# The decays of a state-space layer made in steps, its half-unit on TensorE with all projections in one run, and the next weights' copy moved to the front of ScalarE's half-unit

## The reference, cut to what matters

```python
xn = layernorm(x)
x = x + attention(xn) * silu(moe_ffn(xn))          # 16 heads of 128, linear attention; 8 experts and a shared one
xn = layernorm(x)
x = x + ssm(xn) * silu(quantised_ffn(xn))          # the second layer: the part that the change touches
```

```python
x_t, z_t, b_t, c_t, a_log = split(xn @ W_in.T)     # four projections of 2048 columns and one of 32
decay = exp(-exp(a_log))
def step(states, inp):
    states = states * decay + x_t outer b_t
    y_t = states . c_t + x_t * D
y = layernorm(y * silu(z_t)) * gamma + beta
return y @ W_out.T
```

## Time and profile before

| what | value |
|---|---|
| median of 3 runs | 1784.79 us |
| the profiled execution: its time, and its span from the first to the last instruction | 1785.17 us, 1783.4 us |
| TensorE busy | 1646.7 us (92%) |
| VectorE busy | 1159.3 us (65%) |
| ScalarE busy | 760.0 us (43%) |
| GpSimd busy | 665.3 us (37%) |
| mean granted clock of TensorE | 0.974 |
| batch 0: FFN1 from about 433, the SSM stage from about 496 to about 833 | us from the span's start |
| batch 1: FFN1 from about 1320, the SSM stage from about 1383 to about 1720 | us from the span's start |

### The profile page before, as it was taken

The page is one execution under the profiler, slowest core; times in us unless marked ns, Lnnn a source line. Parts: engine busy times, 40 slices in busy tenths (PEclk is TensorE's granted clock), DMA queues, the critical chain, the costliest instruction groups (busy, mean ns, idle before and its releaser), DMA issues.

```text
span 1783.4 us, 29629 instructions
## 1 busy us (share of the span) xinstructions
PE 1646.7 (92%) x11068; PEld 1364.0 (76%) x11068; DVE 1159.3 (65%) x2041; ACT 760.0 (43%) x1393; POOL 665.3 (37%) x500
## 2 busy tenths in 40 slices
PE   5997899898899999999969978998989999999988
PEld 3886677787788888787938866776868788888878
DVE  4333788663667788886743347886536677777767
ACT  4343445433344444444633434554334344444445
POOL 1453444200225544444515534441012244444535
PEclk9998999999999999999979989999999999999999
DMA  2333000000244434441023320100002443443400
GB/s 77 96 112 118 18 36 1 1 1 10 71 138 143 122 119 129 135 128 49 13 71 104 112 110 19 36 1 1 1 10 71 160 125 119 137 136 120 138 29 25
DMA packets 60062, 135.68 MB, mean 76 GB/s; under 512 B 8129, under 2 KB 12737, under 8 KB 59409
## 3 DMA queue, kind: packets, MB, share of 16 engines
q1 hardware_dynamic: 59920, 133.79, 23.8%
HBM read 130.81 MB, written 2.95 MB: 75 GB/s over the span
## 4 chain that ended last, share of the span: by engine, by line
PE 67%; DVE 12%; POOL 7%; issue 6%; ACT 5%; DMA 2%; SPq 1%; POOLq 0%; DVEq 0%; ACTq 0%
PE ps L549 31%; PE ps L606 6%; PE ps L868 4%; PE ps L645 4%; PE ps L892 4%; PE ps L830 3%; POOL silu_g L449 3%; PE ps L904 3%; PE ps L585 3%; POOL rb L467 2%; POOL fw_lo L434 2%; PE ps L879 2%; PE ps L747 2%; PE ps L748 2%; DVE hid L1343 2%
## 5 line engine op out<-in xcount | busy, mean ns | idle before, releaser
L549 PE MATMUL ps<-xnT_hi,w_in_hi 128*128 128x512 f32 x512 | 222.6, 435 | 0.2 <-issue 0.2
L549 PE MATMUL ps<-xnT_lo,w_in_hi 128*128 128x512 f32 x512 | 203.7, 398 | 0.0
L549 PE MATMUL ps<-xnT_hi,w_in_lo 128*128 128x512 f32 x512 | 202.8, 396 | 0.0
L467 POOL TENSOR_TENSOR rb<-ra,rb 128x512 f32<-128x512 f32 x80 | 117.5, 1469 | 205.1 <-DVE rb L1533 205.1
L425 POOL TENSOR_TENSOR w_in_lo<-w_raw,w_in_hi 128x1024 fp32r<-128x1024 f32 x32 | 83.8, 2620 | 274.5 <-ACT w_in_hi L950 274.5
L1343 DVE TENSOR_TENSOR hid<-ps,silu_g 128x512 f32<-128x512 f32 (+1 forms) x80 | 55.1, 689 | 170.2 <-POOL silu_g L449 106.0
L1654 DVE TENSOR_TENSOR_SCAN lmat<-dec,ident 128x512 f32<-128x512 f32 x128 | 161.3, 1300 | 0.0
L549 PE MATMUL ps<-xnT_hi,fw_hi 128*128 128x512 f32 x312 | 127.8, 410 | 17.3 <-DVE fw_lo L1361 9.8
L512 POOL TENSOR_TENSOR yt<-yg,sz 128x512 f32<-128x512 f32 x64 | 83.5, 1304 | 154.4 <-ACT sz L1261 143.9
L434 POOL TENSOR_TENSOR fw_lo<-fw_raw,fw_hi 128x512 fp32r<-128x512 f32 (+1 forms) x56 | 62.5, 1117 | 186.1 <-ACT fw_hi L980 135.5
L549 PE MATMUL ps<-xnT_hi,fw_lo 128*128 128x512 f32 x312 | 125.1, 401 | 0.0
(11 more groups left out here) (194 smaller groups left out, 4394.6 us busy)
## 6 DMA issues: line engine op xcount, KB each, us to landing
dec<-dec_dram SPq DMA_DIRECT2D x64, 512.0 KB, 4.0
w_raw<-in_w_in SPq DMA_DIRECT2D x32, 512.0 KB, 4.9
wdec<-dec_dram SPq DMA_DIRECT2D x128, 128.0 KB, 4.0
pdec<-dec_dram SPq DMA_DIRECT2D x128, 128.0 KB, 3.8
fw_raw<-in_fw SPq DMA_DIRECT2D x40, 384.0 KB, 3.2
w_raw<-in_w_qkv SPq DMA_DIRECT2D x8, 768.0 KB, 4.2
comb<-comb_dram SPq DMA_DIRECT2D x8, 512.0 KB, 3.8
w_out<-in_w_o SPq DMA_DIRECT2D x2, 2048.0 KB, 10.7
```

Of the source, the lines that this page charges most:

```text
L467: nc.gpsimd.tensor_tensor(rb[:, k], ra[:, k], rb[:, k], ALU.add).then_inc(a_rot.sem, 1)
L549: mm = nc.tensor.matmul(out, left(l, k), right(r, k), start=(j == 0), stop=(j == len(steps) - 1))
```

## The change

It has four parts. On SyncE the first pair's weights are sent ahead of the decays' tables. On GpSimd `decay_suffix` waits for `f_hid` ahead of each step, one step to a half-unit of FFN1; on VectorE `decay_prefix` is split, its small operations after half-unit 3 and its scans after half-units 4 and 5. On TensorE all four projections stand in one run, ahead of the transposes and all the fp32 matmuls. On ScalarE `ssm_prep` moves to the front of the even half-units of pairs 1 to 14, for pair 0 behind the copy of the transposed b; c's copy and the silu of z move ahead of the transposed x.

```diff
--- before.py
+++ after.py
@@ -382,6 +382,7 @@
                 for k in range(2, NF1):
                     ffn_weights(b, NF0 + k, a["fw1"][k].bitcast(F32))
 
+                weights(split_ssm(b, 0), a["w_in"][0], KT * XZBC)
                 sp.wait_ge(s_prep, 5 * (b + 1))
                 sp.dma_start(dec_dram[0], dec_t[:]).then_inc(dec_out, 16)
                 sp.dma_start(dec_dram[1], dec_p[:]).then_inc(dec_out, 16)
@@ -390,7 +391,8 @@
                 sp.wait_ge(dec_out, 48 * (b + 1))
                 for h in range(HP):
                     n = b * HP + h
-                    weights(split_ssm(b, h), a["w_in"][h], KT * XZBC)
+                    if h > 0:
+                        weights(split_ssm(b, h), a["w_in"][h], KT * XZBC)
                     if h == 2:
                         sp.wait_ge(o_mm.sem, o_mm.done(b * NC + NC - 1))
                         sp.dma_start(w_out[:], a["w_out"]).then_inc(w_out_in, 16)
@@ -493,10 +495,12 @@
 
                     w = dec_w[:].rearrange("p (c t) -> p c t", t=P)
                     pool.wait_ge(s_dec.sem, s_dec.done(b))
+                    pool.wait_ge(f_hid.sem, f_hid.done(2 * (b * NF + NF0)))
                     nc.gpsimd.memset(w[:, :, P - 1:P], 1.0)
                     nc.gpsimd.tensor_copy(w[:, :, 0:P - 1], dec_t[:].rearrange("p (c t) -> p c t", t=P)[:, :, 1:P]).then_inc(suffix_step, 1)
                     for k in range(SUFFIX - 1):
                         reach = 1 << k
+                        pool.wait_ge(f_hid.sem, f_hid.done(2 * (b * NF + NF0) + 1 + k))
                         pool.wait_ge(suffix_step, SUFFIX * b + k + 1)
                         nc.gpsimd.tensor_tensor(w[:, :, 0:P - reach], w[:, :, 0:P - reach], w[:, :, reach:P], ALU.mult).then_inc(suffix_step, 1)
                 decay_suffix()
@@ -911,18 +915,17 @@
                     if ahead:
                         project_x(u + 1)
                         project_b(u + 1)
+                        project_c(u + 1)
+                    project_z(u)
+                    if ahead:
                         x_turn(u + 1)
                     unit_intra(u)
-                    if not ahead:
-                        project_z(u)
-                        unit_from_states(u)
-                        return
-                    project_c(u + 1)
-                    b_turn(u + 1)
+                    if ahead:
+                        b_turn(u + 1)
                     unit_from_states(u)
-                    project_z(u)
-                    unit_scores(u + 1)
-                    unit_updates(u + 1)
+                    if ahead:
+                        unit_scores(u + 1)
+                        unit_updates(u + 1)
 
                 u = 2 * b * HP
                 for hf in range(2):
@@ -1269,6 +1272,9 @@
                 def ssm_unit(u):
                     h, hf = u // 2 - b * HP, u % 2
                     ahead = u < 2 * HP * (b + 1) - 1
+                    early = hf == 0 and 1 <= h and h + 1 < HP
+                    if early:
+                        ssm_prep(h + 1, (h + 1) % 2)
                     if ahead:
                         x_copy(u + 1)
                     if u > 2 * b * HP:
@@ -1276,12 +1282,12 @@
                     if not ahead:
                         return
                     b_copy(u + 1)
+                    c_copy(u + 1)
+                    z_silu(u)
                     xtok_copy(u + 1)
-                    if hf == 0 and h + 1 < HP:
-                        ssm_prep(h + 1, (h + 1) % 2)
-                    c_copy(u + 1)
                     btok_copy(u + 1)
-                    z_silu(u)
+                    if h == 0 and hf == 0:
+                        ssm_prep(1, 1)
                     if u < 2 * b * HP + NC:
                         c = u - 2 * b * HP
                         if c == 0:
@@ -1632,20 +1638,21 @@
                     hidden(b, NF0 + k, hf, f_silu, 2 * (b * NF + NF0 + k) + hf, together=last)
                     hidden_lo(b, NF0 + k, hf, s_gu[0:rows, k, 1:2], rows)
 
-                def decay_prefix():
+                def prefix_starts():
 
                     starts = dec_t[:].rearrange("p (c t) -> p c t", t=P)[:, :, 0:1]
                     dve.wait_ge(s_dec.sem, s_dec.done(b))
+                    nc.vector.memset(dec_s[:], 0.0).then_inc(s_prep, 1)
                     dve.wait_ge(suffix_step, SUFFIX * b + 1)
-                    nc.vector.memset(dec_s[:], 0.0).then_inc(s_prep, 1)
                     dve.wait_ge(s_prep, 5 * b + 1)
                     nc.vector.tensor_copy(dec_s[:].rearrange("p (c t) -> p c t", t=P)[:, :, 0:1], starts).then_inc(s_prep, 1)
                     dve.wait_ge(s_prep, 5 * b + 2)
                     nc.vector.memset(starts, 0.0).then_inc(s_prep, 1)
+
+                def prefix_scan(hf):
+                    toks = slice(hf * HALF, (hf + 1) * HALF)
                     dve.wait_ge(s_prep, 5 * b + 3)
-                    for hf in range(2):
-                        toks = slice(hf * HALF, (hf + 1) * HALF)
-                        nc.vector.tensor_tensor_scan(dec_p[:, toks], dec_t[:, toks], dec_s[:, toks], 0.0, ALU.mult, ALU.add).then_inc(s_prep, 1)
+                    nc.vector.tensor_tensor_scan(dec_p[:, toks], dec_t[:, toks], dec_s[:, toks], 0.0, ALU.mult, ALU.add).then_inc(s_prep, 1)
 
                 def decay_scan(u, h):
                     if h == 0:
@@ -1731,8 +1738,10 @@
                     ffn1_unit(u)
                     if u // 2 + 1 < NF1:
                         weights_lo1(b, u // 2 + 1, u % 2)
-                    if u == 1:
-                        decay_prefix()
+                    if u == 3:
+                        prefix_starts()
+                    if u in (4, 5):
+                        prefix_scan(u - 4)
                     if u >= 2 * NF1 - 2:
                         decay_scan(u0, u - (2 * NF1 - 2))
                 for hf in range(2):
```

## The result

The changed kernel took 1840.46 us (median of 6 runs, 1833.31 to 1853.59), the kernel before 1783.47 beside it (6 runs, 1782.47 to 1785.3): a ratio of 1.0332 (95% interval 1.0307 to 1.0356). It is slower by 57 us. Forecast were 1827.0 us in a range of 1798 to 1856: the sign, the mechanism and the range held, and the sum was 13.5 us too low.

What follows compares the result with a forecast made beforehand. The tensor engine, never kept waiting in the SSM stage, was taken to bound the kernel; the change puts a longer loop there. 1785.2 + 49.4 - 2.4 + 3.8 - 9.0 = 1827.0 us, range 1798 to 1856.

Steps and rivals of the forecast that it cites:

- The loop (part 2): SSM stage: early weights' copy waits for its transfer, closing a scans-to-scans loop of 22.54 us; 26 x 1.90 = +49.4.
- dec and wdec sent and landed, up to bTw: First loop step, after the even half-unit's scans: SyncE issues both, wdec lands in 4.0; 5.00 us.
- GpSimd's turn: Even half-unit's scans: GpSimd's y_sum takes its turn between the two scans; 1.2 us, bounds 0 and 1.28.
- Part 1: Tensor engine's order, SSM stage: one projection run instead of three saves 0.40 us per head; six unlooped heads give -2.4.
- my lower bound: Tensor engine's order: a saving of 0 if each new seam among 4-byte matmuls costs what an old one did.
- Part 3: First head of each batch: later weights' copy delays the next projections; +1.9 us per batch, +3.8, bounds 0 and 2.5.
- Part 4: FFN1: GpSimd's decays in steps save a net 4.5 us per batch, -9.0; bounds 2 and 7 per batch.
- The waits for xT: Expected sign: tensor engine waits at the x transposes of even half-units, 2.2 us, 26 times.
- That the copy costs nothing: Rival: SSM transfer early enough that the tensor engine sets the pace; 1767 us, chance 0.08.
- The light loop: Rival: SSM loop binds lightly, GpSimd's turn beside the scans; about 1791 or 1808 us, part below 1805 has chance 0.10.
- The longer loop: Rival: wdec and weights land later in the SSM loop, 23.3 us; about 1853 us, above 1848 has chance 0.08.
- The clock: Rival: granted clock falls in the new SSM waits; +2 to +4 us per head, 1880 to 1930, chance 0.04.

Runs made afterwards that it cites:

- e7: The changed kernel with the 16 affine sums of batch 0 standing two by two in the odd half-units only; 1837.60 us.
- e1: The changed kernel with SyncE sending the next head's weights a half-unit earlier, between the head's two half-units; 1781.56 us.
- e5: The kernel before with only the new half-unit order, ScalarE's weights' copy behind the c copy in all heads, decays in one block; 1774.89 us.
- e6: The changed kernel with the weights sent a half-unit earlier and ScalarE's weights' copy behind the c copy in every head; 1773.16 us.
- e3: The kernel before with only the decays in steps, one GpSimd product per FFN1 half-unit, prefix starts and scans later; 1776.61 us.
- e10: The changed kernel with mt's products ahead of the x transposes and run twice in even half-units of heads 1 to 14; 1843.26 us.
- e4: The kernel before with only ScalarE's copy of the next weights put first in the even half-unit, heads 2 to 15; 1908.55 us.

## Why the prediction was right, and where 13 us are missing

**The loop (part 2) held, member by member.** The means over the 24 heads of the changed kernel in which both ends of the loop are in the trace, beside the forecast's steps, in us:

| step | forecast | measured |
|---|---|---|
| dec and wdec sent and landed, up to bTw | 5.00 | 5.36 |
| bTw and scans, odd half-unit | 2.94 | 2.94 |
| SyncE's queue ahead of the weights | 2.88 | 2.99 |
| landing, to the copy's start | 4.90 | 4.94 |
| copy, x, y square, b | 2.65 | 2.55 |
| gap, bTw and scans, even half-unit | 2.99 | 3.04 |
| GpSimd's turn beside these scans | 1.20 | 1.18 |
| sum | 22.56 (in the text 22.54) | 23.00 |

In batch 1, heads 2 to 14 took 22.55 us each (two half-units, mean); the forecast was 22.54. That it meets to 0.01 is luck: measured from scans to scans, single heads of that batch took 21.7 to 24.4, and the forecast's steps sum to 22.56. That the steps meet one by one is not. GpSimd's turn, an estimate between 0 and 1.28, shows in the rows: the two scans took 3.47 instead of 2.33, and GpSimd's y_sum beside them 2.19 instead of 1.28. The Trainium skill, GPSIMD Engine Reference, section Specifications, has GpSimd share its path to SBUF with vector instructions that read two SBUF inputs. The scans read dec and the constant, both in SBUF, and these rows agree; bTw, which reads PSUM and one SBUF input, took 0.69 with GpSimd at work and without. The same skill's fit for a transfer (DMA: Bandwidth & Descriptors, section Anatomy of one DMA), from which the forecast worked out an estimate of 3.2 us, is one for GpSimd's queue. It doesn't carry over to this transfer on SyncE's queue, which took 4.8.

**The step that failed is the first one of the loop, in batch 0.** There heads 2 to 14 took 23.33 us, 0.8 more than in batch 1. In eight of them the scans' end was followed by bTw after 6.08 us, because what the vector engine does in between (cTp, yg, mt, two affine sums, state updates) takes longer than wdec's landing; the rows 723.37 to 729.45 above show it without a gap. My step took wdec's landing as what ends last and looked at no half-unit of the vector engine with an affine sum in it. Less the 5.00 of the other sixteen, eight times 1.09 make 8.7 us, of which e7 showed 7.5 in the step and 3 in the time (about 6 against its own batch 1). Three more times in batch 0 SyncE sent the weights 0.4 to 1.4 us late (2.7 in sum). Its rows show there that sending itself took longer: 2.53 and 1.99 us for the two pieces of wdec instead of 1.12, and 1.68 for those of pdec instead of 1.23. Why is open.

**Part 1 was a quarter of its size.** The term of 0.20 per half-unit measured 0.05 (half-units of e1 and e5, from 10.15 + 10.49 to 10.10 + 10.44 us). Two beginnings of runs went, as said, but my lower bound, that new seams cost what old ones did, was nearer than the value I took. In the 26 heads that the loop sets this changed nothing. The six others gained 1.2 us instead of 2.4, and most of that is not the seams but the wait of 0.94 us in each batch's last half-unit, which went with the new order. The forecast had said that the tensor engine is never kept waiting in this stage, and had read only the waits ahead of the projections for it.

**Part 3, the first head,** cost 3.4 us per batch instead of 1.9. The copy and the subtraction came as worked out (copy at 511.73, 8.4 us into the half-unit, subtraction until 515.20, wait 1.85 us). The closeness is in part chance, since the pieces that the forecast names add up to 8.7 and not to its 8.4. But behind that wait the engine ran at 1.2 GHz:

```profile
515.31 0.60 PE L553 MATMUL ps<-xnT_hi,w_in_hi 128*128 128x512 f32 x1 [1.85 <-issue]
```

```profile
515.30:518.90 3.60, 3.59 (x9) 2.85 (x10) 0.89 (x4) 0.83 (x2) 1.75 (x2) 0.53 0.02 5
```

The window's columns are those of the earlier trace rows; the granted clock is 0.53. Here, outside the loop, that counts in full: 1.5 per batch more, +3.0. e6 has neither.

**Part 4, the decays,** gave 3.1 per batch in the changed kernel and 3.7 in e3's, not 4.5. The wait of 4.9 us became one of 2.1, as forecast, with a product of GpSimd still beside the second hidT_lo. But counted from the stage's start the third tile's projections began 4.9 and 5.4 us earlier, not 7.0. Then 1.4 us were lost again by the last tile, where I had 2.5, with a wait of 0.9 at the fifth. In batch 0 another 1.2 us went in the stage's last stretch, 7.2 us at a granted clock of 0.80 where before it was 6.0 at 1.00. The rows of the changed kernel, GpSimd, the vector engine, the tensor engine's wait and the window behind it:

```profile
446.69 1.87 POOL L505 TENSOR_TENSOR dec_w<-dec_w 32x1016 f32<-32x1016 f32 x1 [1.83 <-DVE hid L1349]
```

```profile
447.40 1.72 DVE L1358 SCALAR_TENSOR_TENSOR hidT_lo<-hid,s_gu,hidT_hi 128x512 fp32r<-128x512 f32 x1 [0.79 <-ACT hidT_hi L975]
```

```profile
PE ps L553 <- DVE fw_lo L1367: 2.1, 1, 2.1
```

```profile
446.20:450.40 4.20, 4.20 (x12) 3.28 (x13) 2.46 (x3) 1.03 (x2) 1.87 (x1) 0.62 0.02 4
```

The granted clock was 0.62 there, and had been 0.51 behind the longer wait. My rhythm of 4.23 us per half-unit was that of the full clock; 4.2 us at 0.62 cost 1.6 more, and by that the third tile came late: 10.1 us after the wait's end, where the forecast had 8.5.

**The sum.** Against the forecast's +41.8, the profiled execution has +58.6, 16.8 more: 9.9 in the 26 heads of the loop (59.3 instead of 49.4, of which the affine sums are 8.7), 3.0 in the first heads, 1.2 in the six others, 2.8 in FFN1, and -0.1 elsewhere. The profiled execution stands 3.3 us above the median.

**The signs.** The waits for xT came 26 times, as said, at a mean of 1.7 us instead of 2.2. ScalarE's copy had 8.2 us of idle time ahead of it on average (214 us over 26) instead of about 5: in the head shown above ScalarE had run out of work at 708.09, 1.9 us before the half-unit began (709.99), and the transfer was sent only 1.9 us into it.

**The rivals.** That the copy costs nothing is excluded by the result, and e1 shows the condition that it needed: an earlier send. The light loop would have needed GpSimd's turn to fall outside the scans; it fell into them. (The forecast's second sum for it, half of the turn, is 1812 by its own terms and not 1808.) The longer loop came true in batch 0 alone, by another member than I had named. The clock did fall in five of the 26 waits, and it did not set the time: e10, with one such stretch in its loop heads instead of five, has the same stages. The Trainium skill, TensorE: Matmul & The Clock Gate, section HAM oscillation, describes a loop of another kernel in which the clock is halved anew behind every wait for a transfer, waits longer than nearly all of those here. In the changed kernel it was one wait in five, and behind it the slower matmuls only used up slack that the loop left. In e4, with waits of 3.0 us on average, it was 20 of 28, and there the time shows it.

## What to carry to other kernels

Before an instruction is moved to the head of an engine's queue, ask when the transfer it waits for is sent, and behind what: an early place for the reader is worth nothing without an early place for the sender, and everything behind the reader pays. When a wait closes a ring over several engines, add up the ring's members and not the tensor engine's work; filling the wait then gives nothing back, and only a shorter ring does. In e4 the ring's other members came to wait for the tensor engine's work behind its wait, and then that engine and its clock were in the ring. Among the members take, for each step, the later of all that can end it, in every kind of half-unit, side work like the affine sums included.
